# The eight stores that gather the second tile's diagonal blocks: issued by POOL's queue in place of SyncE's

## What is computed

```python
q = l2norm(silu(conv(x @ Wq.T))) / 128 ** 0.5      # conv: 4 taps along the tokens
k = l2norm(silu(conv(x @ Wk.T)))                   # 2 keys and values per token: 256 steps
v = silu(conv(x @ Wv.T))
def step(state, inp):
    q_t, k_t, v_t, g_t, b_t = inp
    state = state * exp(g_t)
    v_new = (v_t - k_t @ state) * b_t
    state = state + outer(k_t, v_new)
    return state, q_t @ state
o = rms_norm(o) * o_norm_w * silu(x @ Wg.T)
x = x + o @ Wo.T
```

## Time and profile before

| | |
|---|---|
| median of 3 runs | 607.36 us (607.34 to 610.03) |
| the profiled execution | 607.52 us, its span 605.7 us |
| PE busy | 555.8 us, 92% of the span |
| DVE busy | 453.8 us, 75% |
| ACT busy | 356.3 us, 59% |
| POOL busy | 39.5 us, 7% |
| DMA queue of SP | 12.1% of 16 engines' span, 17.66 MB |

### The profile page before, as it was taken

One profiled execution on the slowest core, in us unless ns is written; L12 is line 12 of the kernel. 1 busy time (PEld: TensorE's weight loads), 2 busy tenths in 40 slices (PEclk: granted clock), 3 DMA queues, 4 the chain that ended last, 5 costly groups with the idle time before them and its releaser, 6 DMA issues.

```text
span 605.7 us, 15275 instructions
## 1 busy us (share of the span) xinstructions
PE 555.8 (92%) x6440; PEld 374.1 (62%) x6440; DVE 453.8 (75%) x1064; ACT 356.3 (59%) x557; POOL 39.5 (7%) x69
## 2 busy tenths in 40 slices
PE   3879879999999999999999999999998989577997
PEld 1526337576757675766576667667665778465646
DVE  5658898797969787887788778878796525689563
ACT  1567575496559565946694668465864143287351
POOL 5341000100010001000100010010000000100000
PEclk9979999999999999999999999999997899968899
DMA  5001112101210211020002100210013300000002
GB/s 165 1 1 45 27 16 67 27 1 28 59 26 7 34 46 24 10 70 11 22 14 67 13 19 16 66 13 18 2 36 97 97 5 12 0 1 1 1 1 69
DMA packets 49700, 18.63 MB, mean 31 GB/s; under 512 B 39100, under 2 KB 48352, under 8 KB 49632
## 3 DMA queue, kind: packets, MB, share of 16 engines
q1 hardware_dynamic: 49632, 17.66, 12.1%
HBM read 14.49 MB, written 3.15 MB: 29 GB/s over the span
## 4 chain that ended last, share of the span: by engine, by line
PE 75%; DVE 13%; ACT 8%; issue 2%; DMA 1%; ACTq 0%; DVEq 0%
PE bank L1292 18%; PE bank L1342 7%; DVE acc L895 6%; PE bank L1468 5%; PE bank L1245 4%; PE bank L1472 4%; PE bank L1563 4%; PE bank L1345 3%; PE bank L1484 3%; PE bank L1361 3%; PE bank L1478 2%; PE bank L1480 2%; PE bank L1482 2%; PE bank L1427 2%; PE bank L1339 2%
## 5 line engine op out<-in xcount | busy, mean ns | idle before, releaser
L895 DVE SCALAR_TENSOR_TENSOR acc<-bank,cw,acc 128x508 f32<-128x508 f32 (+2 forms) x240 | 176.0, 738 | 37.1 <-ACT acc L597 32.8
L1292 PE MATMUL bank<-xnT,wq 128*128 128x512 f32 x320 | 156.5, 616 | 13.6 <-DVE acc L895 12.8
L1292 PEld LDWEIGHTS bank<-xnT,wq 128*128 128x128 f32 x320 | 57.2, 194 | 72.9 <-issue 45.0
L597 ACT ACTIVATE acc<-bank,cw 128x512 f32<-128x512 f32 x80 | 55.4, 692 | 55.4 <-PE bank L1292 55.3
L1342 PE MATMUL bank<-kq 128*128 128x384 f32 x128 | 50.2, 498 | 0.8 <-issue 0.8
L644 ACT ACTIVATE T<-bank 32x512 f32<-32x512 f32 (+1 forms) x32 | 18.9, 590 | 43.6 <-PE bank L1361 29.8
L612 ACT ACTIVATE vT<-acc 128x512 f32<-128x512 f32 x32 | 21.0, 669 | 37.5 <-DVE acc L895 37.4
L928 DVE SCALAR_TENSOR_TENSOR AM<-bank,rb,DT 128x384 f32<-128x384 f32 x64 | 37.7, 607 | 2.4 <-PE bank L1342 2.1
L1468 PE MATMUL bank<-xnT,wg 128*128 128x512 f32 x64 | 33.8, 655 | 0.0
L996 DVE SCALAR_TENSOR_TENSOR xres<-bank,f,xres 128x256 f32<-128x256 f32 x64 | 26.9, 477 | 8.6 <-PE bank L1472 8.3
L612 ACT ACTIVATE kq<-acc 128x512 f32<-128x512 f32 x48 | 31.3, 659 | 3.2 <-DVE acc L895 2.9
(11 more groups left out here) (245 smaller groups left out, 1076.7 us busy)
## 6 DMA issues: line engine op xcount, KB each, us to landing
wq<-in_w_qkv SPq DMA_DIRECT2D x8, 640.0 KB, 4.0
blocks<-AM SPq DMA_DIRECT2D x128, 8.0 KB, 1.5
xres<-in_x SPq DMA_DIRECT2D x2, 512.0 KB, 4.6
Yl<-in_y_init SPq DMA_DIRECT2D x8, 128.0 KB, 2.4
Bl<-blocks SPq DMA_DIRECT2D x8, 128.0 KB, 2.0
wg<-in_w_gate SPq DMA_DIRECT2D x8, 128.0 KB, 2.1
solved<-Yl SPq DMA_DIRECT2D x8, 128.0 KB, 2.1
Yc<-solved SPq DMA_DIRECT2D x64, 16.0 KB, 1.9
```

Of the source, the lines that this page charges most:

```text
L597: a(acc[:, u % RING, :, :], bank[6 + u % 2][:, :].rearrange("p (b l) -> p b l", b=4), ACT.Copy, scale=cw[:, t, 3:4]).then_inc(s_tap.next(f ...
L895: stt(w, ps[:, :, 0:L - s], cw[:, t, 3 - s:4 - s], w, ALU.mult, ALU.add).then_inc(s_cv.next(f"u{u}_{s}"), 1)
L1292: ins = mm(bank[6 + u % 2][:, :], wq[:, cc, t, :], xnT[:, cc, 512 * half:512 * half + 512], start=cc == 0, stop=cc == KC - 1)
```

## The change

The stores of the second tile move from `gather` on SP into a new function `gather_later` on POOL, with a semaphore of their own, `later_blocks_in_dram`. SP waits for both semaphores before it loads `Bl`. On POOL the function is called in the loop after the decay rows of head h+1 and ahead of the clearing for head h, and once after the loop for head 7. Sources, destinations and sizes of the stores are the same.

```diff
-        s_sc = Signal(sem("blocks_in_dram"), [f"{c}{q}" for c in range(2) for q in range(NB)], 16)
+        s_sc = Signal(sem("blocks_in_dram"), [f"{q}" for q in range(NB)], 16)
+        s_sc2 = Signal(sem("later_blocks_in_dram"), [f"{q}" for q in range(NB)], 16)
...
-                for c, name in enumerate(("e1_7", "e2_3")):
-                    sp.wait_ge(prep.emptied(name).sem, prep.emptied(name).at(name, h))
-                    for q in range(NB):
-                        r = slice(SUB * q, SUB * q + SUB)
-                        dst = blocks[CH * q + B * c:CH * q + B * c + B].rearrange("b k i -> k b i")
-                        sp.dma_start(dst, AM[r, :, 4 * c, r]).then_inc(s_sc.next(f"{c}{q}"), 16)
-                sp.wait_ge(s_sc.sem, s_sc.at(f"1{NB - 1}", h))
+                sp.wait_ge(prep.emptied("e1_7").sem, prep.emptied("e1_7").at("e1_7", h))
+                for q in range(NB):
+                    r = slice(SUB * q, SUB * q + SUB)
+                    dst = blocks[CH * q:CH * q + B].rearrange("b k i -> k b i")
+                    sp.dma_start(dst, AM[r, :, 0, r]).then_inc(s_sc.next(str(q)), 16)
+                sp.wait_ge(s_sc.sem, s_sc.at(str(NB - 1), h))
+                sp.wait_ge(s_sc2.sem, s_sc2.at(str(NB - 1), h))
                 sp.dma_start(Bl[:, :, :], blocks[:, :, :]).then_inc(s_bl.next("b"), 16)
...
+            def gather_later(h):
+
+                AM = AMs[h % 2][:, :, :].rearrange("p b (c n) -> p b c n", n=P)
+                pool.wait_ge(prep.emptied("e2_3").sem, prep.emptied("e2_3").at("e2_3", h))
+                for q in range(NB):
+                    r = slice(SUB * q, SUB * q + SUB)
+                    dst = blocks[CH * q + B:CH * q + CH].rearrange("b k i -> k b i")
+                    g.dma_start(dst, AM[r, :, 4, r]).then_inc(s_sc2.next(str(q)), 16)
             for h in range(H - 1):
                 pool.wait_ge(prep.fills.sem, prep.fills.at("dt2", h))
                 decay_rows(h + 1)
+                gather_later(h)
                 pool.wait_ge(post.fills.sem, post.fills.at("ly", h))
                 pool.wait_ge(s_yd.sem, s_yd.at("yd", h))
                 g.tensor_tensor(Yc[:, :, SUB:BLK], T16[:, :, SUB:BLK], T16[:, :, SUB:BLK], ALU.add).then_inc(s_z.next("z"), 1)
 
+            gather_later(H - 1)
             pool.wait_ge(tail.fills.sem, tail.fills.at("wo3", H - 1))
```

## The result

| | before | changed |
|---|---|---|
| median | 607.35 us (4 runs, 605.05 to 610.03) | 625.07 us (4 runs, 622.97 to 626.88) |
| the profiled execution | 607.52 us, span 605.7 | 625.99 us, span 624.2 |
| PE busy | 555.8 us, 92% | 562.6 us, 90% |
| POOL busy | 39.5 us | 72.7 us |

The ratio is 1.0289, with a 95% interval of 1.0234 to 1.0344: slower by 17.7 us. The kernel was timed twice more with the experiments, at 1.0276 (1.0225 to 1.0327) and 1.0255 (1.0219 to 1.0292).

The account below looks back on a forecast made before the run. TensorE, busy 92%, was taken to bound the kernel. Delays of 0 (head 0), 10.1 (heads 1 to 5), 5.5 (head 6), 13.6 (head 7) and 3 us (clock) sum to 32.2 us on 607.52: 640 us, range 619 to 665.

Parts of the forecast that it names:

- the order on POOL: Sign: POOL's first store of head 1 follows the decay rows, not the tile; head 7's do not start before 471.
- DVE's wait for `Bl`: Sign: DVE's wait for the block load grows from 2.1 us in two to about 41 us in seven.
- The start on POOL: POOL is free for the moved stores only after clearing and decay rows: 114.42 in head 1, 471.89 in head 7.
- c = 1.0 us: Price of one store issue on POOL, eight per head, set between SP's 0.43 us and POOL's longest loop instruction, 1.91 us.
- The rival of the quick issue: POOL's issue nearly as quick as SP's; at c = 0.43, 620 us; range 613 to 626, chance 0.17.
- From the last issue to the substitution: From POOL's last store issue to DVE's first substitution: 1.11 us to the load's issue plus 2.08 us, together 3.19 us.
- Heads 0 to 6: Head 0 hidden, 0; heads 1 to 5 lose 2.0 us each, 10.1 us; head 6 loses 5.5 us.
- Head 7: Substitution moves from 466.12 to 483.08, evacuations of `ly` end at 488.20, PE's step at 474.63 is late: 13.6 us.
- The clock: After head 7's stall of 13 us PE runs at half clock over work now at 2.4 GHz: 3 us more.
- the rule that was weighed: Issuing from several engines saves only issue time; by it alone the change gains: the not-slower rival, 605.4 us, chance 0.03.
- the lock between DVE and GpSimd: DVE's two-port modes keep GpSimd from writing descriptors; expected to cost nothing, otherwise part of the slow-issue rival, chance 0.23.
- the cover of 0.75 us: Heads 1 to 5: DVE's convolution of unit 4 ends at 129.49, PE needs its bank at 130.24; 0.75 us absorbs delay.

Follow-up runs that it names:

- the split run: The changed kernel with each of POOL's eight stores per head cut into two, sixteen issues per head; 648.50 us, ratio 1.0626.
- the experiment that frees head 7 alone: The changed kernel with only head 7's POOL stores put ahead of the clearing for head 6; 611.95 us, ratio 1.0046.
- The first experiment: The changed kernel with POOL's eight stores of head h+1 put ahead of the clearing for head h; 609.33 us against 608.75 us, ratio 0.999.

## Why the prediction was right, and where its sum was off

It said slower, 640 us with a range of 619 to 665; measured were 625.1. The mechanism is shown; the size was nearly double (32 us against 17.7), and one term makes most of that. Of its own signs the order on POOL and the longest wait in head 7 came true. Two did not: DVE's wait for `Bl` grew to 20.6 us in five heads, not to 41 in seven, and the issue took half of the 1 us.

- **The start on POOL** held to 0.3 us in head 1 (114.42 forecast, 114.64) and 1.2 in head 7 (471.89, 473.06). Undoing it removes the loss; imposing it on SP brings 11 us of it back.
- **c = 1.0 us is the term that failed**: it is 0.53. I took the middle between SP's 0.43 and POOL's longest instruction and so gave weight to a row that has no likeness to an issue; the nearest row in kind, SP's own issue, was 0.1 us away. With 8c = 4.2 the same steps give 0 for heads 1 to 5 (c is under the 0.75 where they begin to pay), 1.7 for head 6, 9.8 for head 7 and 3 for the clock, 14.5 us: 622. The rival of the quick issue, to which I gave 0.17, is the case that came; by the sum the place in the queue gives the direction at any price.
- **From the last issue to the substitution**, 3.19 us, was short: 1.3 us to the load's issue and 2.26 us behind it in head 7, 3.6 together, and 5.5, 4.7 and 5.1 in heads 2, 4 and 5. There DVE could start only 3.4 to 3.9 us after the load's issue, where in the kernel before all eight landed in 1.9 to 2.1. That makes the 0.35 to 1.10 us of waiting in these heads, where the sum at 0.53 us had a cover of 1.0. Why they landed late is not shown; their place in time alone does not tell it, since in the split run all eight landed in 1.9 to 2.3 us.
- **Heads 0 to 6**: 3.2 us in the experiment that frees head 7 alone, against the 1.7 of the sum at c = 0.53 and the 15.6 of the prediction. The profiled pair hides this part: PE's gate matmuls of phase 6 are 3.6 us late (451.73, 455.30), but at the clearing only 1.2 are left; in between the kernel before was granted 0.50 from 464 to 472, the changed one 0.79.
- **Head 7**: PE's step came 11.3 us late, 1.2 of it already there at the clearing; 10.0 against 9.8 at c = 0.53 (13.6 in the prediction). With the 3.2 of the other heads and 3.5 for the clock that is 16.7 of the 17.7 us.
- **The clock**, 3 us: 8.9 us in the profiled pair, 3.5 us (1 to 6) over the timed runs. The term was about right for the time. It was an estimate from one profile, and single profiles of this stretch differ by up to 6.6 us in kernels without a stall, so part of that is luck.
- **Against the rule that was weighed.** Stores from two queues at once would have gained what the wait of 2.1 us is worth if POOL had been free. The first experiment is that case, and no gain can be measured (0.999). The Trainium skill, "DMA: Bandwidth & Descriptors", Issuing engines are not separate DMA queues, says that this saves only issue time, and the trace agrees: head 1's load went out 3.1 us earlier. The first byte that the Trainium skill, "DMA: Bandwidth & Descriptors", Specifications, puts near 1 us against 0.6 us would have misled as a price of the issue: the rows show 0.53 against 0.43, and 1.7 against 1.5 us from issue to landing. Of the lock between DVE and GpSimd, which the prediction weighed by the Trainium skill, "SBUF — State Buffer", SBUF: two separate sides, no run here shows anything: the median and the shortest of 64 issues are both 528 ns.
- **Open**: the 6 us between the sum at 8.07 us of issues and the run with split stores (38 against 32). Its waits for the load are 2.9 us longer than the sum's; the half clock behind a longer stall and the cover of 0.75 us, of which the extra waits of up to 1.4 us per head have none left, are further candidates; none was separated.

No version beats the kernel before. The one with the stores ahead of the clearing equals it.

## What to carry to other kernels

The queue of an engine that is busy for 39.5 of 606 us can still be the wrong place for a transfer: look at what it stands waiting for when the data is ready, and put the new instructions ahead of that wait, not behind it. Price the place before the instruction: here eight issues at 0.53 us were harmless in one position and cost some 17 us in the other, nearly all of it in the one phase without other work. For an issue that the trace does not show, take the issue of another engine as the nearest row, and a wide range.

## What the runs showed of the hardware

- An issue on POOL's queue held POOL for 528 ns with 128 runs of 64 bytes and 512 ns with 64 runs; SP's took 432 ns in the median. From issue to landing: 1.7 us against 1.5 us.
- The same load of 128 KB landed 1.9 to 2.1 us after its issue in all eight heads of the kernel before, 1.9 to 3.8 us in the changed one, where it goes out later, and 1.9 to 4.1 us in the first experiment, where it goes out earlier; the cause is not shown.
- In all six profiles in which PE had stood still for 3.75 to 15.3 us before the step, the granted clock over the next ten us of dense work was 0.50; in the six without such a stall, fillers included, it was 0.67 to 1.00. Over the whole stretch to the end of `wo3` kernels without a stall still took 49.9 to 56.5 us, with less than full clock in some executions: one profiled pair is not enough to price the clock.
